# Own-key maxima packed into full banks, exponent floors moved to ScalarE, and a new planned order of instructions

## The chip, the cores and the metric

One NeuronCore of a Trainium2 chip runs the whole program. The metric is device time in microseconds (us) of one launch. The kernel before takes 598.94 us, the median of 3 runs (597.7 to 599.84). Its engines are TensorE (PE in the profile, PEld for its weight loads), VectorE (DVE), ScalarE (ACT), GpSimd (POOL) and SyncE (SP), which issues DMAs.

## The reference

A transformer block on x of 2048 rows by 128 columns: layer norm, then attention and a quantised feed-forward layer side by side, both added to x.

```python
xn = _layernorm(x, axis=-1)
# attention: 16 heads of 8 columns
scores = jnp.einsum('bhqd,bhkd->bhqk', q, k) * scaling
scores = scores + _power_law_mask(S, scores.dtype)[None, None]
attn = jax.nn.softmax(scores, axis=-1)
out = jnp.einsum('bhqk,bhkd->bhqd', attn, v)
# feed-forward: fp4_linear quantises both operands in blocks of 16 to 0, .5, 1, 1.5, 2, 3, 4, 6
h = jax.nn.silu(fp4_linear(x, w_gate)) * fp4_linear(x, w_up)
return fp4_linear(h, w_down)
```

The mask lets query i see key j where j - i >= 0, and weighs it by 1 / (j - i + 1). So a query sees its own position and all later ones.

## The kernel before

**Tiling.** The 2048 positions are 4 groups of 512 (`GROUPS = [3, 2, 0, 1]`, `GQ = 512`), each 4 tiles of 128. A unit is one group of queries with four heads, so there are 16 units, numbered 0 to 15 in the order of the groups. Every unit is computed twice over.

**First pass, the maxima.** For each unit TensorE forms scores with queries on the partitions (item `max`, lines L1425 and, for the triangle where key equals query block, L1428), and VectorE reduces each bank of PSUM to a row maximum (L1240). For keys of a later group a bank is full (512 columns). For the unit's own group ("own keys") query tile a sees 512, 384, 256 or 128 columns, so its four tiles times four heads make 16 banks and 16 reductions, most of them not full. There are 640 such items. When a unit's maxima are done VectorE folds them (`parts`, L1251 and L1256), GpSimd splits them into three bf16 parts (`minor`, L900 to L904), TensorE turns them (`rows`, L1436), ScalarE copies them (L1056) and a DMA puts them as extra rows under the queries (L679).

**Second pass, the scores.** TensorE forms the scores again with keys on the partitions, less the maximum (item `st`, L1449 and L1452, 640 of them). ScalarE takes the exponential (L1049). It is then multiplied by the distance weights: either by GpSimd, two heads at once and interleaved in the ring (L895), or by VectorE, one head at a time (L1267). `pair_vec` says which; in the kernel before it names VectorE for 97 of 320 pairs. Then TensorE multiplies by the values for four heads at once (`pv`, L1467; eight instructions in the trace, as fp32 goes in two passes). The ring has 8 pairs.

**Feed-forward.** 16 tiles, spread over the run. ScalarE makes the curve (L1017 to L1026), VectorE does nine steps (`silu`, L1202 to L1226), of which the last is max(exponent, 1) times a rounding constant (L1226); GpSimd quantises in three steps (`quant`, L911 to L915); TensorE turns and multiplies (L1389, L1400).

**What sets the order.** `plan()` plays the kernel through with a cost for every item and writes down, for each engine, the order in which items are taken. This order is then fixed in the program; each engine runs its list from the front and waits on semaphores. A pair goes to VectorE where the plan sees GpSimd more than `POOL_QUEUE` behind. A pair on GpSimd is charged `POOL_START + 2 * n * POOL_COL`, with 220 ns and 2.04 ns a column. Maxima are kept ahead of scores by `lead_at`. On TensorE a maximum has rank 4 while fewer than two are ahead, a score 4.5; the lower rank is taken first.

## Time and profile before

| | |
|---|---|
| median of 3 runs | 598.94 us |
| profiled execution, its own time | 599.36 us |
| span in that profile | 597.6 us |
| busy: PE, DVE, ACT, POOL | 562.5, 547.1, 409.3, 503.2 us |

Busy time is the union of an engine's instructions. On PE it includes the pipeline latency of each matmul, so a PE that is busy 94% may still have room. On VectorE an instruction's record goes on while the next one has already begun, so the step from start to start is what one more instruction costs, and is shorter than its mean duration.

### The profile page before, as it was taken

What the parts mean: (1) busy time and instruction counts of PE and PEld (TensorE: products, weight loads), DVE (VectorE), ACT (ScalarE), POOL (GpSimd) and SP (SyncE); (2) the same over time, 40 slices, a digit from 0 to 9 for tenths busy, and PEclk for the clock granted to TensorE, in tenths of its full rate; (3) what the DMA queues carried; (4) which work ended last, traced back from release to release, by engine and by line L of the source; (5) the groups of instructions that cost most, each with busy time, mean ns of one, the idle gap of its engine ahead of it and who ended that gap; (6) DMA issues with size and microseconds to landing.
All of it is one profiled execution on the core that took longest, in us unless ns stands there. A gap on an engine that the chain in (4) does not pass through costs nothing.

```text
span 597.6 us, 11270 instructions
## 1 busy us (share of the span) xinstructions
PE 562.5 (94%) x3791; PEld 247.5 (41%) x3791; DVE 547.1 (92%) x1165; ACT 409.3 (68%) x868; POOL 503.2 (84%) x409
## 2 busy tenths in 40 slices
PE   5999999999899999999999999999999998999995
PEld 4677844544343434333333333342344343343322
DVE  5999989998999899999999999999998989999672
ACT  4668486675665567766776676767666767677793
POOL 7378888797998889798999989897988889798773
PEclk9999999999998999999999999999999999999999
DMA  7434344010000001000000000000000000000000
GB/s 203 103 104 113 110 99 108 2 74 8 1 3 1 2 1 60 39 1 2 1 1 1 20 1 2 1 2 2 1 2 19 2 0 2 2 0 2 2 2 18
DMA packets 14832, 16.66 MB, mean 28 GB/s; under 512 B 1639, under 2 KB 14216, under 8 KB 14360
## 3 DMA queue, kind: packets, MB, share of 16 engines
q1 hardware_dynamic: 14240, 15.70, 9.5%
q8 instruction: 30, 0.49, 0.3%
q10 hardware_dynamic: 536, 0.26, 0.2%
q14 instruction: 26, 0.21, 0.1%
HBM read 11.75 MB, written 4.01 MB: 26 GB/s over the span
## 4 chain that ended last, share of the span: by engine, by line
PE 53%; DVE 27%; issue 7%; ACT 7%; POOL 5%; POOLq 0%; ACTq 0%; DVEq 0%
PE psum L1467 14%; DVE mxp L1240 13%; PE psum L1425 13%; PE psum L1449 10%; DVE ring L1267 4%; PE psum L1310 3%; POOL ring L895 3%; PE psum L1381 2%; ACT ring L1049 2%; PE psum L1400 2%; PE psum L1428 2%; PE psum L1383 1%; PE psum L1452 1%; DVE psum L1222 1%; DVE xw L1218 1%
## 5 line engine op out<-in xcount | busy, mean ns | idle before, releaser
L895 POOL TENSOR_TENSOR ring<-ring,dist 128x1024 f32<-128x1024 f32 (+3 forms) x223 | 398.6, 1815 | 51.6 <-ACT ring L1049 50.8
L1240 DVE TENSOR_REDUCE mxp<-psum 128x1 f32<-128x512 f32 (+3 forms) x640 | 354.7, 598 | 16.6 <-PE psum L1425 13.9
L1049 ACT ACTIVATE ring<-psum 128x512 f32<-128x512 f32 (+3 forms) x446 | 221.8, 557 | 93.5 <-PE psum L1452 46.8
L1425 PE MATMUL psum<-kop,qop 96*128 96x512 bf16 (+3 forms) x640 | 198.4, 352 | 7.2 <-DVE mxp L1240 3.7
L1449 PE MATMUL psum<-qop,kop 128*128 128x512 bf16 (+3 forms) x640 | 191.2, 349 | 7.4 <-DVE mxp L1240 2.8
L1467 PE MATMUL psum<-ring,vaug 128*32 128x512 f32 (+3 forms) x1280 | 155.3, 556 | 2.5 <-POOL ring L895 1.9
L1267 DVE TENSOR_TENSOR ring<-psum,dist 128x512 f32<-128x512 f32 (+3 forms) x194 | 115.1, 620 | 12.0 <-ACT psum L1049 11.4
L1049 ACT ACTIVATE psum<-psum 128x512 f32<-128x512 f32 (+3 forms) x194 | 99.7, 545 | 31.7 <-PE psum L1449 19.0
L1425 PEld LDWEIGHTS psum<-kop,qop 96*128 96x128 bf16 x640 | 56.5, 97 | 134.6 <-DVE mxp L1240 45.5
L1449 PEld LDWEIGHTS psum<-qop,kop 128*128 128x128 bf16 x640 | 59.3, 97 | 83.6 <-DVE mxp L1240 19.7
L1428 PE MATMUL psum<-tri_q,identb 128*128 128x128 bf16 x256 | 55.9, 220 | 0.0
L1452 PE MATMUL psum<-tri_k,identb 128*128 128x128 bf16 x256 | 52.5, 219 | 0.0
L1467 PEld LDWEIGHTS psum<-ring,vaug 128*32 128x32 f32 x1280 | 25.8, 108 | 48.7 <-issue 47.1
L1428 PEld LDWEIGHTS psum<-tri_q,identb 128*128 128x128 bf16 x256 | 25.2, 99 | 13.5 <-issue 1.9
L1310 PE MATMUL psum<-identf 128*128 128x128 f32 x200 | 30.8, 274 | 0.0
L1452 PEld LDWEIGHTS psum<-tri_k,identb 128*128 128x128 bf16 x256 | 25.1, 98 | 7.7 <-issue 0.3
L1310 PEld LDWEIGHTS psum<-identf 128*128 128x128 f32 x200 | 22.4, 141 | 3.5 <-issue 0.5
L1017 ACT ACTIVATE xw<-psum 128x352 f32<-128x352 f32 x16 | 7.4, 464 | 17.1 <-PE psum L1383 17.1
L911 POOL TENSOR_TENSOR xw<-xw 128x352 f32<-128x352 f32 x16 | 15.1, 942 | 3.6 <-DVE xw L1226 3.5
L1056 ACT ACTIVATE mrow<-psum 12x512 bf16<-12x512 bf16 x16 | 9.3, 581 | 11.9 <-PE psum L1436 11.9
L1400 PE MATMUL psum<-wdT,hT 128*128 128x128 f32 (+1 forms) x96 | 15.2, 296 | 1.7 <-ACT hT L1035 1.6
L913 POOL TENSOR_TENSOR xw<-xw 128x352 f32<-128x352 f32 x16 | 15.0, 938 | 1.3
(134 smaller groups left out, 467.9 us busy)
## 6 DMA issues: line engine op xcount, KB each, us to landing
parts_dram<-qpart SPq DMA_DIRECT2D x18, 128.0 KB, 3.4
kop<-parts_dram SPq DMA_DIRECT2D x6, 384.0 KB
qop<-parts_dram SPq DMA_DIRECT2D x6, 384.0 KB
xin<-_attn_hidden_states_dram SPq DMA_DIRECT2D x4, 256.0 KB, 5.0
ring<-inv_dram SPq DMA_DIRECT2D x1, 1024.0 KB, 5.1
out_dram<-xin SPq DMA_DIRECT2D x4, 256.0 KB, 2.3
qop<-parts_dram SPq DMA_DIRECT2D x3, 288.0 KB
kop<-parts_dram SPq DMA_DIRECT2D x3, 288.0 KB
```

The costliest lines, as they stand in the source:

```text
L895: g_.tensor_tensor(slot(p)[:, 0:n], slot(p)[:, 0:n], both, ALU.mult).then_inc(weighed_pool, 1)
L911: g_.tensor_tensor(v, v, c, ALU.add).then_inc(hq_seq, 1)
L1049: a_.activation(scores if pair_vec[p] else slot(p)[:, 0:n, e % 2], scores, ACT.Exp, scale=SCALE).then_inc(exp_done, 1)
L1240: v_.tensor_reduce(mxp[:, u % 2, 4 * a + j, c - g:c - g + 1], bank(*o)[:, 0:n], AX_X, ALU.max).then_inc(max_used, 1)
L1267: v_.tensor_tensor(slot(p)[:, 0:n, e % 2], bank("st", e)[:, 0:n], weights(d, n), ALU.mult).then_inc(weighed_vec, 1)
L1310: nc.tensor.transpose(psum[:, OUT_BANK, 0:P], identf[:], identf[:])
L1400: ins = mm(down_of(i), hT[0:k, i % 2, m], wdT[0:k, m], start=(m == 0), stop=(m == 2))
L1425: ins = mm(bank(*o)[:, 0:n], qop[0:K_MAX, u // NQ % 2, h, P * a:P * (a + 1)], kop[0:K_MAX, h, k0:k0 + n], start=True, stop=(c != g))
L1428: ins = mm(bank(*o)[:, 0:P], identb[:], tri_q[:], start=False, stop=True)
L1449: ins = mm(bank(*o)[:, 0:n], kop[0:K_ST, h, P * b:P * (b + 1)], qop[0:K_ST, u // NQ % 2, h, 0:n], start=True, stop=(d >= TPG))
L1452: ins = mm(bank(*o)[:, P * d:P * (d + 1)], identb[:], tri_k[:], start=False, stop=True)
L1467: ins = mm(psum[32 * j:32 * j + 32, OUT_BANK, 0:n], vaug[:, b, VC * h:VC * h + 32], slot(2 * s + j // 2)[:, 0:n, j % 2], start=(b == NT - ...
```

## The change

The numbers in the plan change: a pair on GpSimd is charged 140 ns and 1.906 ns a column, an item for the exponent floor stands on ScalarE, and past half of the work (`LEAN_AFTER`) a score takes rank 3.9 on TensorE, ahead of a maximum, as long as the lead is kept. Own keys: query tile 1 of a head (384 columns) shares a bank with tile 3 (128), and tile 2 of one head (256) with tile 2 of the next, so a unit has 10 own-key items, each of 512 columns, and 544 items in all. One reduction then gives four maxima, for which `mxp` grows from 4 to 7 columns a row. The last silu step leaves VectorE; ScalarE does it as a Relu and an Identity with bias. A pair that VectorE weighs now lies in the ring as two plain halves instead of interleaved.

```diff
-SILU_STAGES, FP4_STAGES = 9, 6
+SILU_STAGES, FP4_STAGES = 8, 6
+LEAN_AFTER = 0.5
+NMX = NG + 3
+ROW_OF = [0, 2, 1, 3]
-POOL_COL, POOL_START = 2.04, 220
+POOL_COL, POOL_START = 1.906, 140
+def max_pieces(a, j):
+    if a == 1:
+        return [(1, j), (3, j)]
+    if a == 2:
+        return [(2, j), (2, j + 1)] if j % 2 == 0 else []
+    return [(0, j)] if a == 0 else []
...
-        pool(("quant", i), 2700, [("DVE", ("silu", i, SILU_STAGES - 1))], rank=0)
+        act(("floor", i), F, [("DVE", ("silu", i, SILU_STAGES - 1))], n=2, rank=2)
+        pool(("quant", i), 2700, [("ACT", ("floor", i))], rank=0)
...
-                return 4.5
+                late = work["st"] > LEAN_AFTER * total
+                return 3.9 if late and work["max"] >= lead_at(work["st"]) else 4.5
...
-        mxp = sb("mxp", [P, 2, TPG * 4, NG], F32)
+        mxp = sb("mxp", [P, 2, 4, TPG, NMX], F32)
+        def weighted(p, j, n):
+            if pair_vec[p]:
+                return slot(p).rearrange("p n j -> p (n j)")[:, GQ * j:GQ * j + n]
+            return slot(p)[:, 0:n, j]
...
+                if o[0] == "floor":
+                    i = o[1]
+                    act.wait_ge(silu_seq, SILU_STAGES * (i + 1))
+                    a_.activation(fbuf[:, 1], gate_of(i), ACT.Relu, scale=ROUND, bias=rounds[:, 0:1]).then_inc(floor_seq, 1)
+                    act.wait_ge(floor_seq, i + 1)
+                    a_.activation(fbuf[:, 1], fbuf[:, 1], ACT.Identity, bias=rounds[:, 1:2]).then_inc(fround_ready, 1)
...
-                    if k < SILU_STAGES - 1:
-                        ins.then_inc(silu_seq, 1)
-                    else:
-                        v_.tensor_scalar(c, gate, 1.0, ROUND, ALU.max, ALU.mult).then_inc(fround_ready, 1)
+                    ins.then_inc(silu_seq, 1)
...
-                    v_.tensor_reduce(mxp[:, u % 2, 4 * a + j, c - g:c - g + 1], bank(*o)[:, 0:n],
-                                     AX_X, ALU.max).then_inc(max_used, 1)
+                    if c == g and a:
...
+                        v_.tensor_reduce(into, parts, AX_X, ALU.max).then_inc(max_used, 1)
+                    else:
+                        v_.tensor_reduce(mxp[:, u % 2, j, ROW_OF[a], c - g:c - g + 1], bank(*o),
+                                         AX_X, ALU.max).then_inc(max_used, 1)
...
+                        if u + 2 < len(units) and parts_of(u + 2)[2] < parts_of(u)[2]:
+                            vec.wait_ge(mneg_ready, 2 * u + 2)
+                            v_.memset(mxp[:, s, :, :, NG - 1:NG], NEG)
...
-                    ins = mm(bank(*o)[:, 0:n], qop[0:K_MAX, u // NQ % 2, h, P * a:P * (a + 1)],
-                             kop[0:K_MAX, h, k0:k0 + n], start=True, stop=(c != g))
-                    if c == g:
-                        ins = mm(bank(*o)[:, 0:P], identb[:], tri_q[:], start=False, stop=True)
+                    x0 = 0
+                    for b, jj in max_pieces(a, j) if c == g else [(a, j)]:
+                        k0 = P * (TPG * g + b) if c == g else GQ * c
+                        n = GQ * (c + 1) - k0
+                        ins = mm(bank(*o)[:, x0:x0 + n], qop[0:K_MAX, u // NQ % 2, 4 * hq + jj, P * b:P * (b + 1)],
+                                 kop[0:K_MAX, 4 * hq + jj, k0:k0 + n], start=True, stop=(c != g))
+                        if c == g:
+                            ins = mm(bank(*o)[:, x0:x0 + P], identb[:], tri_q[:], start=False, stop=True)
+                        x0 += n
```

**Scores first.** TensorE at the last scores of unit 10, in the second half of the work (`kop,qop` with 512 or 384 columns is a maximum, `qop,kop` a score, `tri_k` and `tri_q` triangles, `ring,vaug` the product with the values). Before, at about score 380 of 640:

```order
L1449 MATMUL psum<-qop,kop 128x128
L1452 MATMUL psum<-tri_k,identb 128x128
L1425 MATMUL psum<-kop,qop 128x512
L1449 MATMUL psum<-qop,kop 128x128
L1452 MATMUL psum<-tri_k,identb 128x128
L1449 MATMUL psum<-qop,kop 128x128
L1452 MATMUL psum<-tri_k,identb 128x128
L1467 MATMUL psum<-ring,vaug 32x384 x4
L1425 MATMUL psum<-kop,qop 128x512
L1425 MATMUL psum<-kop,qop 128x384
```

The changed order, at about score 370:

```order
L1476 MATMUL psum<-kop,qop 128x512
L1519 MATMUL psum<-ring,vaug 32x512 x4
L1501 MATMUL psum<-qop,kop 128x384
L1504 MATMUL psum<-tri_k,identb 128x128
L1501 MATMUL psum<-qop,kop 128x384
L1504 MATMUL psum<-tri_k,identb 128x128
L1501 MATMUL psum<-qop,kop 128x384
L1504 MATMUL psum<-tri_k,identb 128x128
L1519 MATMUL psum<-ring,vaug 32x512 x4
L1501 MATMUL psum<-qop,kop 128x384
L1504 MATMUL psum<-tri_k,identb 128x128
L1501 MATMUL psum<-qop,kop 128x256
```

Where one or two scores stood between maxima, five scores and two products with the values now stand before the next one.

**The last unit's rows.** TensorE behind the turning of unit 15's maxima (`identb,mpart`). Before, 13 scores of unit 14 follow it before unit 15's first; these are the first of them:

```order
L1436 MATMUL psum<-identb,mpart 12x128 x4
L1449 MATMUL psum<-qop,kop 128x512
L1452 MATMUL psum<-tri_k,identb 128x128
L1449 MATMUL psum<-qop,kop 128x384
L1452 MATMUL psum<-tri_k,identb 128x128
```

In the changed order, down to unit 15's first two scores (the last row):

```order
L1488 MATMUL psum<-identb,mpart 12x128 x4
L1449 MATMUL psum<-wdT,hT 128x128 x3
L1519 MATMUL psum<-ring,vaug 32x512 x4
L1501 MATMUL psum<-qop,kop 128x128
L1504 MATMUL psum<-tri_k,identb 128x128
L1501 MATMUL psum<-qop,kop 128x128
L1504 MATMUL psum<-tri_k,identb 128x128
L1519 MATMUL psum<-ring,vaug 32x512 x4
L1501 MATMUL psum<-qop,kop 128x128
L1504 MATMUL psum<-tri_k,identb 128x128
L1501 MATMUL psum<-qop,kop 128x128
L1504 MATMUL psum<-tri_k,identb 128x128
...
L1519 MATMUL psum<-ring,vaug 32x384 x4
L1519 MATMUL psum<-ring,vaug 32x256 x4
L1501 MATMUL psum<-qop,kop 128x512 x2
```

Four scores and four products stand between the turning and unit 15's first score.

**The floor on ScalarE.** One feed-forward tile in the changed order (`xw<-psum,rounds` and `xw<-xw,rounds` are the new pair):

```order
L1085 ACTIVATE ring<-psum 128x512 x7
L1085 ACTIVATE psum<-psum 128x512 x2
L1085 ACTIVATE ring<-psum 128x512
L1060 ACTIVATE xw<-psum,rounds 128x352
L1062 ACTIVATE xw<-xw,rounds 128x352
L1085 ACTIVATE ring<-psum 128x512
```

The exponentials behind the pair wait with it when VectorE's steps are late.

In numbers of the two orders: maxima 640 before and 544 now; pairs on VectorE 97 and 90 (of 512 columns 71 and 65, of 384 columns 12 and 13, of 256 columns 10 and 5, of 128 columns 4 and 7); up to the last maximum VectorE weighs 156 and 146 heads; from the turning of unit 15's maxima on, TensorE has 61 scores and 52.

## Rows read from the trace of the kernel before

**Rows 1.** The page: busy time of the engines, share of the span, instructions.

```profile
PE 562.5 (94%) x3791; PEld 247.5 (41%) x3791; DVE 547.1 (92%) x1165; ACT 409.3 (68%) x868; POOL 503.2 (84%) x409
```

**Rows 2.** Busy by stretch, columns: stretch, length, PE, PEld, DVE, ACT, POOL, PEclk, DMA.

```profile
0.00:60.00 60.00, 53.10 (x375) 38.84 (x376) 52.53 (x151) 39.98 (x68) 39.32 (x85) 1.00 0.49 131
60.00:553.00 493.00, 473.67 (x3151) 195.67 (x3148) 470.55 (x972) 338.70 (x732) 435.93 (x304) 1.00 0.06 17
553.00:597.60 44.60, 35.70 (x269) 12.95 (x267) 24.00 (x46) 30.66 (x69) 27.91 (x21) 1.00 0.03 7
```

**Rows 3.** Waits within 60 to 553 us: who, on whom, total, times, longest.

```profile
DVE mxp L1240 <- PE psum L1425: 13.9, 19, 1.6
...
POOL ring L895 <- ACT ring L1049: 43.7, 39, 4.3
POOL xw L911 <- DVE xw L1226: 3.5, 5, 1.1
POOL mres L900 <- DVE mpart L1256: 2.0, 5, 0.6
...
PEld psum L1425 <- DVE mxp L1240: 45.0, 72, 0.9
```

**Rows 4.** Groups by shape: VectorE's maxima and a weighing (busy, mean ns | idle before).

```profile
L1240 DVE TENSOR_REDUCE mxp<-psum 128x1 f32<-128x512 f32 x448 | 292.0, 679 | 14.5 <-PE psum L1425 13.9
L1240 DVE TENSOR_REDUCE mxp<-psum 128x1 f32<-128x384 f32 x64 | 34.4, 543 | 0.1
L1240 DVE TENSOR_REDUCE mxp<-psum 128x1 f32<-128x256 f32 x64 | 26.0, 412 | 0.9 <-PE psum L1428 0.8
L1240 DVE TENSOR_REDUCE mxp<-psum 128x1 f32<-128x128 f32 x64 | 17.3, 278 | 1.1 <-PE psum L1428 1.1
L1267 DVE TENSOR_TENSOR ring<-psum,dist 128x512 f32<-128x512 f32 x142 | 93.0, 681 | 10.4 <-ACT psum L1049 10.0
```

**Rows 5.** Timeline of VectorE, 332 to 336 us: start, length of the merged piece.

```profile
332.28 0.51 DVE L1226 TENSOR_SCALAR xw<-psum 128x352 f32<-128x352 f32 x1
332.71 0.68 DVE L1267 TENSOR_TENSOR ring<-psum,dist 128x512 f32<-128x512 f32 x1
333.31 1.87 DVE L1240 TENSOR_REDUCE mxp<-psum 128x1 f32<-128x512 f32 x3
335.10 0.41 DVE L1267 TENSOR_TENSOR ring<-psum,dist 128x256 f32<-128x256 f32 x1
335.43 1.27 DVE L1240 TENSOR_REDUCE mxp<-psum 128x1 f32<-128x512 f32 x2
```

**Rows 6.** One line, L1251: shortest, median, longest ns.

```profile
L1251 DVE TENSOR_REDUCE mneg<-mxp x16: 150/183/210, 34.7 to 552.7; 128x16 f32<-128x16 f32 x4, 128x16 f32<-128x32 f32 x4, 128x16 f32<-128x64 f32 x4, 128x16 f32<-128x48 f32 x4
```

**Rows 7.** Groups by shape: ScalarE's steps most like the new pair.

```profile
L1026 ACT ACTIVATE xw<-xw 128x352 f32<-128x352 f32 x16 | 8.1, 507 | 0.0
...
L1022 ACT ACTIVATE xw<-psum 128x352 f32<-128x352 f32 x16 | 7.5, 470 | 0.0
```

**Rows 8.** Groups by shape: GpSimd's pairs, four widths.

```profile
L895 POOL TENSOR_TENSOR ring<-ring,dist 128x1024 f32<-128x1024 f32 x153 | 323.5, 2139 | 46.6 <-ACT ring L1049 45.9
L895 POOL TENSOR_TENSOR ring<-ring,dist 128x768 f32<-128x768 f32 x20 | 32.7, 1648 | 0.8 <-ACT ring L1049 0.8
L895 POOL TENSOR_TENSOR ring<-ring,dist 128x512 f32<-128x512 f32 x22 | 25.4, 1163 | 0.3 <-ACT ring L1049 0.2
L895 POOL TENSOR_TENSOR ring<-ring,dist 128x256 f32<-128x256 f32 x28 | 18.4, 674 | 4.0 <-ACT ring L1049 3.9
```

**Rows 9.** Timeline of GpSimd, from 412 us.

```profile
412.10 6.33 POOL L895 TENSOR_TENSOR ring<-ring,dist 128x1024 f32<-128x1024 f32 x3 [3.12 <-ACT ring L1049]
```

**Rows 10.** Timeline, all engines, 551 to 563 us, rows of the last unit's maxima.

```profile
551.72 0.69 DVE L1240 TENSOR_REDUCE mxp<-psum 128x1 f32<-128x512 f32 x1
...
554.49 0.59 ACT L1056 ACTIVATE mrow<-psum 12x512 bf16<-12x512 bf16 x1 [0.57 <-PE psum L1436]
...
555.10 1.80 SPq L679 DMA_DIRECT2D qop<-mrow  x3
...
562.94 0.62 ACT L1049 ACTIVATE ring<-psum 128x512 f32<-128x512 f32 x1 [0.80 <-PE psum L1449]
```

**Rows 11.** Timeline of TensorE, products with the values, 546 to 560 us.

```profile
546.44 1.11 PE L1467 MATMUL psum<-ring,vaug 128*32 128x512 f32 x8
```

More of the change, by code:

```diff
@@ L174, in plan @@
     for u, (g, hq) in enumerate(units):
-        for a, j in sorted(((a, j) for a in range(TPG) for j in range(4)), key=lambda o: o[1] if u == 0 else 0):
+        for a, j in sorted(((a, j) for a in range(TPG) for j in range(4)),
+                           key=lambda o: o[1] + (o[0] == 2) if u == 0 else 0):
             if True:
                 for c in range(g, NG):
-                    n = GQ - P * a if c == g else GQ
+                    pieces = max_pieces(a, j) if c == g else [(a, j)]
+                    if not pieces:
+                        continue
                     item = ("max", u, a, j, c)
-                    h = 4 * hq + j
+                    h = 4 * hq + pieces[-1][1]
                     if g == GROUPS[0]:
@@ L189, in plan @@
                         needs.append(("DVE", ("parts", u - 2, 1)))
-                    pe(item, n + (P if c == g else 0), needs, rank=6)
-                    vec(item, n, [("PE", item)], rank=6)
+                    pe(item, GQ + (P * len(pieces) if c == g else 0), needs, rank=6)
+                    vec(item, GQ, [("PE", item)], rank=6)
         for k in range(2):
@@ L382, in take @@
             issued["maxed"] += 1
-            work["max"] += TPG - item[2] if item[4] == units[item[1]][0] else TPG
+            work["max"] += TPG
         seen[(engine, item)] = end
@@ L525, in build @@
         moments = sb("moments", [P, NT, 2], F32)
+        rounds = sb("rounds", [P, 2], F32)
         amax = sb("amax", [P, len(PIECES), SC_COLS], F32)
@@ L583, in build @@
         fp4_scaled = sem("fp4_scaled")
+        rounds_ready = sem("rounds_ready")
+        floor_seq = sem("floor_seq")
         scales_zeroed = sem("scales_zeroed")
@@ L1048, in _ @@
                         act.wait_ge(pv_done, (p - SLOTS) // 2 + 1)
-                    a_.activation(scores if pair_vec[p] else slot(p)[:, 0:n, e % 2], scores,
+                    a_.activation(scores if pair_vec[p] else weighted(p, e % 2, n), scores,
                                   ACT.Exp, scale=SCALE).then_inc(exp_done, 1)
@@ L1266, in _ @@
                         vec.wait_ge(pv_done, (p - SLOTS) // 2 + 1)
-                    v_.tensor_tensor(slot(p)[:, 0:n, e % 2], bank("st", e)[:, 0:n], weights(d, n),
+                    v_.tensor_tensor(weighted(p, e % 2, n), bank("st", e)[:, 0:n], weights(d, n),
                                      ALU.mult).then_inc(weighed_vec, 1)
@@ L1467, in _ @@
                         ins = mm(psum[32 * j:32 * j + 32, OUT_BANK, 0:n], vaug[:, b, VC * h:VC * h + 32],
-                                 slot(2 * s + j // 2)[:, 0:n, j % 2], start=(b == NT - 1), stop=(b == TPG * g))
+                                 weighted(2 * s + j // 2, j % 2, n), start=(b == NT - 1), stop=(b == TPG * g))
                     ins.then_inc(pv_done, 1)
```

30 lines of the change are left out of this document (21 added, 9 removed).

## The prediction, made before the result was known

> **What bounds the kernel now.** I read the busy shares first [rows 1]. TensorE shows 94%, VectorE 92%, GpSimd 84%, ScalarE 68%. The first figure must not be taken at its word, as a matmul's record holds its latency; the waits tell more. So next the stretches [rows 2]: up to 553 us VectorE is busy 470.6 of 493 us (95%), and behind 553 us, when the last maximum is out, only 24 of 44.6. Then who waits for whom [rows 3]: in the 493 us VectorE waits 13.9 us for TensorE's maxima, while TensorE's weight loads wait 45.0 us for VectorE to free a bank. GpSimd waits 43.7 us for exponentials, so it has room. Up to 553 us the bound is VectorE, in order and almost without holes. Behind it comes a tail of 43 us from the copy of unit 15's rows at 554.49 to the end [rows 10], which scores, exponentials and products set and VectorE does not.
>
> **VectorE, part by part.** What one more instruction costs there is the step from start to start, not the duration. From the timeline [rows 5]: three full reductions begin at 333.31 and the next instruction at 335.10, so 0.597 us each; 256 columns take 0.33 (335.10 to 335.43); L1226 with 352 columns 0.43 (332.28 to 332.71). The mean durations fall by 0.133 us for each 128 columns [rows 4], which gives steps of 0.464 for 384 and 0.20 for 128.
> Packing: 64 x (0.464 + 0.33 + 0.20) = 63.6 us of partial reductions become 96 full ones, 57.3 us: -6.3. That four results instead of one cost nothing more is my assumption; if each cost 0.1 us again, the gain would be 0, and below -6.3 there is nothing to be had, since no column goes.
> Floor: 16 x 0.43 = -6.9.
> Folding: L1251 takes 150 ns for 16 numbers and 210 for 64 [rows 6], 1.25 ns each. It now always reads 112 instead of 40 on average: +0.09 us, 32 times (L1256 alike): +2.9. Two small memsets: +0.3.
> Weighings up to the last maximum: 512 columns 116 to 108, 384 columns 18 to 20, 256 columns 14 to 6, 128 columns 8 to 12: -4.8 + 0.9 - 2.6 + 0.8 = -5.7.
> Together -15.7 us. The plain halves in the ring change nothing that I can see: with the interleaved output a weighing of 512 columns takes 681 ns and a reduction with one result 679 [rows 4]; bounds 0 to -1 us for the products that read them.
> The Trainium skill's "VectorE: DVE Perf Modes", section "The DRAIN you can't avoid", says that the next operation does not start before the pipe is empty. By that every instruction would cost its whole duration and packing would save 64 x (0.543 + 0.412 + 0.278) - 96 x 0.679 = 13.7 us, an estimate with that page's rule and durations of rows 4. The timeline speaks against it here, since a full reduction's successor starts 0.08 us before its record ends.
>
> **GpSimd takes over.** A pair of 512 columns steps by (6.33 - 2.14) / 2 = 2.095 us [rows 9]; the other widths, their durations less 0.044, 1.60, 1.12 and 0.63 [rows 8]. It gets 6 more of 512, 1 fewer of 384, 5 more of 256 and 3 fewer of 128: +14.7 us. Up to the last rows it is 12.1 us, and the quantising of tile 15 (2.8 us) now stands before them too: +14.9. In 60 to 553 us GpSimd is busy 435.9, free 57.1: 43.7 waiting for exponentials, 8 for others [rows 3], 5.4 in gaps. If the stretch shrinks to 477.3, it has 26.5 free, 13.4 of which stay, so its waits for exponentials must fall from 43.7 to 13.1.
> Why they should fall: the old plan charges 2.309, 1.787, 1.264 and 0.742 us for the four widths, against real steps of 2.095, 1.60, 1.12 and 0.63. Over 153, 20, 22 and 28 pairs it charges 42.7 us too much, almost exactly what GpSimd waits: the exponentials stand in the order where a slower GpSimd would want them. The new charge of 2.092 us for 512 columns is right. I do not take the whole of it, since three engines now have to fit at over 90%: waits of 19 us, GpSimd ends 6 us behind VectorE's saving: +6. Ends: 0 and the rival below.
>
> **The floor on ScalarE.** Its nearest steps take 470 and 507 ns [rows 7], about 1.0 us with the wait between them, 16 us in all on an engine busy 338.7 of 493 us: hidden. But the chain from VectorE's last step to GpSimd is longer by about 0.5 us, and GpSimd already waits there 5 times, 3.5 us [rows 3]. Queued behind the pair on ScalarE are exponentials, for which GpSimd and VectorE wait in turn. Between 0 and 16 x 0.5 = 8 us; I take +1.5, as two thirds of the tiles had slack.
>
> **TensorE.** As many matmuls and columns as before: 0. Its real load is a product of four heads at about 1.04 us (1.11 with its latency [rows 11]), and it spends 45 us waiting for VectorE [rows 3], time that comes free when banks do.
>
> **The tail.** From the copy at 554.49 unit 15's first exponential comes 8.45 us later, at 562.94, and the end 34.7 us after that [rows 10]. TensorE had 13 scores to do between; it now has four short ones and four products (about 1.04 + 1.04 + 0.8 + 0.6 us) and the down product, some 4.5 us. The three DMAs are issued by 556.90, 2.4 us after the copy's start; their landing isn't in the rows, so the gap is between 2.4 and 8.45 us. I take 5.4, near the work that stands there: -3. What stood there is done earlier, where VectorE bounds. The alternation of pairs in unit 15: 0, between -2 and +2. The start, where loads and the first chain rule: 0, between -2 and +2.
>
> **Sum.** 597.6 - 15.7 + 6 + 1.5 - 3 = 586.4 us of span. The profiled execution took 599.36, 1.8 over its span, which gives 588.2, and it lies 0.4 above the median: 587.8, so 588 us.
>
> **Rivals.**
> 1. GpSimd becomes the bound and keeps its waits. Its stretch is then 450.8 busy + 57.1 free = 507.9 instead of 493: 597.6 + 14.9 + 1.5 - 3 = 611, about 612 us. For it: its work grows while everybody else's shrinks. Against it: an engine that bounds has its supply waiting, and the overcharge accounts for the waits. It turns to a loss when the waits fall by less than 13 of 43.7 us. Chance 0.08.
> 2. GpSimd and VectorE bound in turns: the waits fall by about 15 to 20 us only. 593 to 599 us. Chance 0.17.
> 3. Scores first starve VectorE. In the second half I count, with the steps above, 14 stretches of over 2 us of other work on TensorE between two maxima, against 7 before, and one of them stands in the order shown. At most three maxima are ahead, 1.8 us of VectorE's time. Seven more holes of 1 us: about 595 us. Against it: VectorE has weighings and silu steps in them, and the lead is asked for first. Chance 0.10.
> 4. All is carried over, GpSimd fits: 597.6 - 15.7 - 3 = 578.9 and 1.4 more, 580 us. Chance 0.10. Each instruction at its full duration would end there as well: 7.4 us below my forecast, 580.5 us. Rows 5 speak against that; chance 0.03.
> My own case, 582 to 593 us, has 0.52. The Trainium skill's rule on the drain, above, is the one that would give the 580.5.
>
> **The numbers.** 588 us. Eight in ten lie between 579 and 599 us: below is half of rival 4, above rival 1 and the end of rival 2. This measurement can tell about 0.3% (1.8 us) from no change. Faster by more (below 597.1): 0.83, which is my case, rival 4, and most of 2 and 3. Within: 0.07, the ends of 2 and 3. Slower: 0.10, rival 1 and 0.02 for mishaps of 3.
>
> **What would show it.** Right: VectorE's reductions of 512 columns with four results at about 680 ns and 0.60 apart; no L1226; its last maximum at 538 to 546 us instead of 551.7; GpSimd's wait for exponentials near 20 us and its share at 88 to 90%; unit 15's first exponential about 5 us behind the last copy of rows. Wrong: reductions with four results over 750 ns; VectorE waiting for maxima over 25 us; GpSimd waiting 35 us or more with its last `minor` no earlier than now.

## The result and the profile after

The changed kernel takes 604.79 us (median of 4 runs, 603.11 to 607.01) against 598.43 us for the kernel before: ratio 1.0094 [1.0064, 1.0123]. Forecast were 588 us, with 0.10 for slower. The span in the profile is 603.3 us against 597.6. The page, its busy line (against [rows 1]) and its chain of waits, and below it the chain of the kernel before:

```profile
PE 559.9 (93%) x3791; PEld 250.0 (41%) x3791; DVE 530.7 (88%) x1041; ACT 422.7 (70%) x900; POOL 516.0 (86%) x418
...
PE 47%; POOL 26%; ACT 12%; issue 5%; DVE 4%; DMA 2%; SPq 1%; ACTq 1%; POOLq 0%; DVEq 0%
```

```profile
PE 53%; DVE 27%; issue 7%; ACT 7%; POOL 5%; POOLq 0%; ACTq 0%; DVEq 0%
```

The chain that ended last ran over VectorE for 27% before and over GpSimd for 26% now.

The savings on VectorE are real: 547.1 us have become 530.7, 16.4 less where 15.7 were forecast. By stretch, as [rows 2]:

```profile
0.00:60.00 60.00, 49.49 (x331) 34.95 (x332) 48.18 (x124) 37.15 (x60) 33.72 (x82) 0.97 0.48 127
60.00:553.00 493.00, 471.03 (x3184) 200.24 (x3181) 458.36 (x871) 352.22 (x766) 447.94 (x314) 1.00 0.06 18
553.00:610.00 57.00, 39.35 (x282) 14.82 (x278) 24.18 (x48) 33.36 (x74) 34.38 (x24) 0.93 0.02 6
```

In the first 60 us all four engines do less than before: TensorE 49.5 instead of 53.1, VectorE 48.2 instead of 52.5, GpSimd 33.7 instead of 39.3. The waits within 60 to 553 us, as [rows 3]:

```profile
POOL ring L923 <- ACT ring L1085: 31.1, 27, 3.2
PEld psum L1476 <- DVE mxp L1287: 23.6, 36, 0.9
DVE mxp L1287 <- PE psum L1476: 19.1, 30, 1.9
...
POOL xw L903 <- DVE hT L1198: 5.9, 3, 2.0
...
DVE mxp L1287 <- PE psum L1479: 3.8, 6, 1.3
```

TensorE's weight loads wait 23.6 us for VectorE instead of 45.0, and GpSimd's wait for exponentials falls from 43.7 to 31.1. The waits that were to shrink did shrink, and the kernel still is slower. VectorE by groups (as [rows 4]: busy, mean ns, idle before), then ScalarE's new pair (against [rows 7]):

```profile
L1287 DVE TENSOR_REDUCE mxp<-psum 128x1 f32<-128x512 f32 x448 | 289.8, 678 | 24.5 <-PE psum L1476 19.1 <-PE psum L1479 4.8
L1316 DVE TENSOR_TENSOR ring<-psum,dist 128x512 f32<-128x512 f32 x130 | 84.9, 681 | 15.4 <-ACT psum L1085 14.9
L1285 DVE TENSOR_REDUCE mxp<-psum 128x4 f32<-128x512 f32 x96 | 64.3, 678 | 3.6 <-PE psum L1479 3.4
```

```profile
L1062 ACT ACTIVATE xw<-xw,rounds 128x352 f32<-128x352 f32 x16 | 9.4, 588 | 0.5
L1060 ACT ACTIVATE xw<-psum,rounds 128x352 f32<-128x352 f32 x16 | 8.9, 559 | 1.4 <-DVE psum L1258 1.1
```

A reduction with four results (L1285) takes 678 ns, as long as one with one result. VectorE's timeline shows the step from start to start: 1.20 us for the two at 25.49, 0.60 each.

```profile
25.49 1.28 DVE L1285 TENSOR_REDUCE mxp<-psum 128x4 f32<-128x512 f32 x2
26.69 0.68 DVE L1287 TENSOR_REDUCE mxp<-psum 128x1 f32<-128x512 f32 x1
27.29 0.68 DVE L1285 TENSOR_REDUCE mxp<-psum 128x4 f32<-128x512 f32 x1
```

**Where the time went.** I took the start of the first exponential of each unit from ScalarE's timelines, which sets both runs side by side:

| first exponential of unit | 0 | 1 | 2 | 4 | 8 | 11 | 13 | 15 | end |
|---|---|---|---|---|---|---|---|---|---|
| before | 48.4 | 76.1 | 93.2 | 118.4 | 229.2 | 395.1 | 486.8 | 562.9 | 597.6 |
| after | 50.7 | 86.2 | 104.0 | 130.6 | 239.2 | 402.4 | 489.8 | 567.1 | 603.3 |
| later by | 2.3 | 10.1 | 10.8 | 12.2 | 10.0 | 7.3 | 3.0 | 4.2 | 5.7 |

The whole loss, and more, is made before unit 4. Behind that point the changed kernel needs 472.7 us where the one before needed 479.2. The 2.3 us of the first column may be scatter: over all profiles of this study unit 0's first exponential comes between 47.5 and 52.5 us, and between 47.5 and 52.1 in the eight that share the changed kernel's order. So the table of the experiments counts from there, in two parts: the start up to unit 4's first exponential (79.9 us against 70.0) and the rest. Together they explain 3.4 of the 6.4 us between the medians; the other 3 lie ahead of the first exponential or in scatter, which one profile of a kernel can't tell apart.

TensorE's granted clock goes with that scatter. In the changed kernel TensorE stood idle for 2.16 us before 40.06, waiting for a DMA of `kop`, and shortly after the clock was at half (1.2 GHz) for 3.4 us:

```profile
35.00:41.30 6.30, 4.14 (x34) 3.11 (x32) 5.52 (x12) 3.81 (x10) 2.23 (x2) 1.00 0.25 81
41.30:44.70 3.40, 3.40 (x17) 2.45 (x16) 3.03 (x7) 0.89 (x2) 3.00 (x7) 0.50 0.28 77
```

Of the eight profiles in this order the three with such a fall ahead of unit 0's first exponential (the changed kernel, e9, e11) have it at 50.4 to 52.1 us, the other five at 47.5 to 49.8. Whether the fall delays it, or both follow a late DMA, no run settles. It doesn't make the late start: e7's clock stays at 1.00 throughout, and its start is as long.

**The mechanism of the start.** Unit 1 can't go on until the ring of 8 pairs empties, which takes unit 0's first product with the values. It comes some 26 us behind unit 0's first exponential before and 34 us in the changed kernel. Here is TensorE at that place, before (L1371 turns a chunk of the quantised input, L1467 is the product; it is the timeline, columns start, length):

```profile
61.80 0.61 PE L1371 MATMUL psum<-identf,xw 128*128 128x128 f32 x4
...
70.80 0.60 PE L1371 MATMUL psum<-identf,xw 128*128 128x128 f32 x4
...
74.58 1.10 PE L1467 MATMUL psum<-ring,vaug 128*32 128x512 f32 x8
...
77.30 0.66 PE L1371 MATMUL psum<-identf,xw 128*128 128x128 f32 x4
```

And after (L1420 turns, L1519 is the product), then ScalarE, which has the copy of the turned chunk (L1036) queued ahead of its next exponential:

```profile
78.39 0.63 PE L1420 MATMUL psum<-identf,xw 128*128 128x128 f32 x4 [0.33 <-DVE mxp L1287]
...
84.16 0.63 PE L1420 MATMUL psum<-identf,xw 128*128 128x128 f32 x4 [0.31 <-DVE mxp L1287]
84.71 1.11 PE L1519 MATMUL psum<-ring,vaug 128*32 128x512 f32 x8
```

```profile
84.82 0.60 ACT L1036 ACTIVATE xnT<-psum 128x512 f32<-128x512 f32 x1 [5.17 <-PE psum L1420]
86.23 1.67 ACT L1085 ACTIVATE ring<-psum 128x512 f32<-128x512 f32 x3 [0.82 <-PE psum L1504]
```

In both orders two turns stand ahead of the first product. A turn needs the quantised chunk from GpSimd, which waits for VectorE's six steps on each piece of the input (the row L903 <- L1198 of the waits above, 5.9 us), and a bank of PSUM, which VectorE frees with a reduction. At 84.16 both came within 0.15 us of each other, GpSimd's last step at 84.01 and the reduction, which the profile names, at 84.15. Either way it is VectorE's row. The last of its six steps (L1162, now L1198) on the first two chunks, before:

```profile
52.17 0.68 DVE L1162 TENSOR_SCALAR hT<-psum 128x512 f32<-128x512 f32 x1
...
59.34 0.68 DVE L1162 TENSOR_SCALAR hT<-psum 128x512 f32<-128x512 f32 x1
```

and after:

```profile
73.73 0.68 DVE L1198 TENSOR_SCALAR hT<-psum 128x512 f32<-128x512 f32 x1
...
79.50 0.67 DVE L1198 TENSOR_SCALAR hT<-psum 128x512 f32<-128x512 f32 x1
```

The first chunk is 21.6 us late, the second 20.2. In between VectorE reduces maxima of units 3 and 4. Own keys are now 10 items and not 16, so the plan gets through each unit's maxima with fewer items, and it places maxima of units further ahead where pieces of the input stood. By the order, TensorE now turns the four chunks behind scores 16, 16, 24 and 36, before behind 6, 16, 18 and 27.

The place of the second turn is not what decides. In e7 (below) the first product stands ahead of it, and the start is as long:

```profile
81.33 1.11 PE L1519 MATMUL psum<-ring,vaug 128*32 128x512 f32 x8
82.60 0.63 PE L1420 MATMUL psum<-identf,xw 128*128 128x128 f32 x4 [0.16 <-DVE mxp L1287]
```

What goes with the length of the start is how many maxima VectorE has taken by the first product. The busy time of its reductions up to there, before (L1240) and after (L1285, then L1287):

```profile
0.00:74.58 74.58, 31.88 (x71) 1.00 0.46 126
```

```profile
0.00:84.71 84.71, 19.44 (x30) 0.98 0.47 124
0.00:84.71 84.71, 20.35 (x32) 0.98 0.47 124
```

That is 31.9 against 39.8 us. If the units are taken in turn, 7 of the 71 reductions are unit 4's before, and 22 of the 62 after. The same count for other orders (steps are an estimate from those of rows 5; the product counts from unit 0's first exponential):

| | reductions | their steps, us | first product after | start |
|---|---|---|---|---|
| before | 71 | 29.6 | 26.1 | 70.0 |
| changed | 62 | 37.0 | 34.0 | 79.9 |
| e7_old_charge, e12_packing_floor | 62 | 37.0 | 33.4 | 81.1 |
| e6_heads | 57 | 34.0 | 33.6 | 79.7 |
| e5_fp4_first | 59 | 35.2 | 31.0 | 77.5 |
| g2_held2 | 51 | 30.4 | 29.4 | 77.1 |
| g1_held1 | 47 | 28.1 | 25.7 | 71.4 |

The plan also places the first product behind the last of 200 filling transposes, in every order. Their own time is not what holds it: e8 leaves out half of them, and the product comes no sooner (34.5 us). No run changes the count of maxima alone; that they hold the product back is read from the seven orders and from the turns' waits.

### The profile page after: what moved, and what is told of

Its sections match the earlier page's. It is cut to its first block, busy times and chain, and to the rows that moved or that the text cites. A ratio compares the mean times of both kernels' runs of the same rounds, so it can differ in the third digit from the quotient of the medians.

```text
span 603.3 us, 11188 instructions
## 1 busy us (share of the span) xinstructions
PE 559.9 (93%) x3791; PEld 250.0 (41%) x3791; DVE 530.7 (88%) x1041; ACT 422.7 (70%) x900; POOL 516.0 (86%) x418
## 4 chain that ended last, share of the span: by engine, by line
PE 47%; POOL 26%; ACT 12%; issue 5%; DVE 4%; DMA 2%; SPq 1%; ACTq 1%; POOLq 0%; DVEq 0%
POOL ring L923 20%; PE psum L1519 15%; PE psum L1476 10%; PE psum L1501 10%; ACT ring L1085 4%; PE psum L1449 2%; DMA kop<-parts_dram 2%; PE psum L1430 2%; POOL xw L941 2%; POOL xw L939 2%; POOL xw L943 1%; PE psum L1432 1%; PE psum L1504 1%; DVE mxp L1287 1%; ACT kop L959 1%
## 5 line engine op out<-in xcount | busy, mean ns | idle before, releaser
L923 POOL TENSOR_TENSOR ring<-ring,dist 128x1024 f32<-128x1024 f32 (+3 forms) x230 | 412.4, 1822 | 37.1 <-ACT ring L1085 36.8
L1287 DVE TENSOR_REDUCE mxp<-psum 128x1 f32<-128x512 f32 x448 | 289.8, 678 | 24.5 <-PE psum L1476 19.1
L1085 ACT ACTIVATE ring<-psum 128x512 f32<-128x512 f32 (+3 forms) x460 | 229.1, 562 | 89.7 <-PE psum L1504 43.9
L1476 PE MATMUL psum<-kop,qop 96*128 96x512 bf16 (+3 forms) x640 | 194.3, 351 | 7.3 <-DMA kop<-parts_dram 2.2
L1501 PE MATMUL psum<-qop,kop 128*128 128x512 bf16 (+3 forms) x640 | 188.2, 349 | 4.7 <-DVE ring L1316 1.6
L1519 PE MATMUL psum<-ring,vaug 128*32 128x512 f32 (+3 forms) x1280 | 156.5, 555 | 8.8 <-POOL ring L923 7.1
L1316 DVE TENSOR_TENSOR ring<-psum,dist 128x512 f32<-128x512 f32 (+3 forms) x180 | 105.0, 616 | 19.6 <-ACT psum L1085 18.9
L1476 PEld LDWEIGHTS psum<-kop,qop 96*128 96x128 bf16 x640 | 58.8, 98 | 104.2 <-DVE mxp L1287 23.6
L1085 ACT ACTIVATE psum<-psum 128x512 f32<-128x512 f32 (+3 forms) x180 | 89.7, 542 | 10.8 <-PE psum L1504 5.3
L1285 DVE TENSOR_REDUCE mxp<-psum 128x4 f32<-128x512 f32 x96 | 64.3, 678 | 3.6 <-PE psum L1479 3.4
L1504 PE MATMUL psum<-tri_k,identb 128*128 128x128 bf16 x256 | 52.1, 218 | 0.0
L1519 PEld LDWEIGHTS psum<-ring,vaug 128*32 128x32 f32 x1280 | 26.4, 108 | 57.5 <-issue 55.6
L1479 PE MATMUL psum<-tri_q,identb 128*128 128x128 bf16 x256 | 48.2, 221 | 0.0
L941 POOL TENSOR_TENSOR xw<-xw 128x352 f32<-128x352 f32 x16 | 14.9, 930 | 1.3
L1449 PE MATMUL psum<-wdT,hT 128*128 128x128 f32 (+1 forms) x96 | 14.9, 291 | 1.0 <-ACT hT L1071 0.9
```

The lines of the kernel that those rows point to most:

```text
L923: g_.tensor_tensor(slot(p)[:, 0:n], slot(p)[:, 0:n], both, ALU.mult).then_inc(weighed_pool, 1)
L1085: a_.activation(scores if pair_vec[p] else weighted(p, e % 2, n), scores, ACT.Exp, scale=SCALE).then_inc(exp_done, 1)
L1285: v_.tensor_reduce(into, parts, AX_X, ALU.max).then_inc(max_used, 1)
L1287: v_.tensor_reduce(mxp[:, u % 2, j, ROW_OF[a], c - g:c - g + 1], bank(*o), AX_X, ALU.max).then_inc(max_used, 1)
L1316: v_.tensor_tensor(weighted(p, e % 2, n), bank("st", e)[:, 0:n], weights(d, n), ALU.mult).then_inc(weighed_vec, 1)
L1476: ins = mm(bank(*o)[:, x0:x0 + n], qop[0:K_MAX, u // NQ % 2, 4 * hq + jj, P * b:P * (b + 1)], kop[0:K_MAX, 4 * hq + jj, k0:k0 + n], start= ...
```

## The experiments

Each kernel was timed in 3 rounds beside the kernel before, whose own median was 598.1 to 599.4 us in these series; the ratio is to the one beside it. e2, e3, e9, f2 and f4 leave a part of the computation out. "Start" is from the first exponential of unit 0 to that of unit 4 in its profile, "rest" from there to the end of the span.

| kernel | median us | ratio to before | start | rest |
|---|---|---|---|---|
| before | 598.43 | 1 | 70.0 | 479.2 |
| changed | 604.79 | 1.0094 [1.0064, 1.0123] | 79.9 | 472.7 |
| e1_interleaved | 605.60 | 1.0106 [1.0079, 1.0132] | 80.0 | 473.7 |
| e2_pool_short | 599.90 | 1.0030 [1.0011, 1.0049] | 79.9 | 468.3 |
| e3_dve_short | 604.00 | 1.0084 [1.0054, 1.0114] | 78.9 | 473.3 |
| e4_no_lean | 614.69 | 1.0273 [1.0246, 1.0300] | 79.9 | 481.4 |
| e5_fp4_first | 598.05 | 0.9989 [0.9973, 1.0004] | 77.5 | 469.4 |
| e6_heads | 605.37 | 1.0100 [1.0075, 1.0126] | 79.7 | 476.0 |
| e7_old_charge | 607.01 | 1.0126 [1.0096, 1.0155] | 81.1 | 473.4 |
| e8_half_fill | 602.92 | 1.0075 [1.0046, 1.0103] | 80.4 | 473.6 |
| e9_both_short | 595.40 | 0.9946 [0.9929, 0.9963] | 78.9 | 464.3 |
| e10_floor_vec | 604.49 | 1.0105 [1.0085, 1.0125] | 79.9 | 473.4 |
| e11_unpacked | 605.71 | 1.0120 [1.0090, 1.0149] | 80.1 | 473.3 |
| e12_packing_floor | 611.96 | 1.0215 [1.0196, 1.0235] | 81.1 | 478.5 |
| f1_new_charge | 600.67 | 1.0032 [1.0019, 1.0045] | 70.9 | 479.6 |
| f2_dve_short | 593.72 | 0.9924 [0.9907, 0.9942] | 69.8 | 472.0 |
| f4_pe_short | 571.27 | 0.9543 [0.9521, 0.9565] | 67.3 | 453.5 |
| f5_lean | 606.10 | 1.0118 [1.0094, 1.0142] | 69.9 | 484.3 |
| g1_held1 | 602.33 | 1.0056 [1.0035, 1.0076] | 71.4 | 475.7 |
| g2_held2 | 604.01 | 1.0096 [1.0072, 1.0120] | 77.1 | 475.3 |

### Which engine bounds: work taken away in a fixed order

**f2_dve_short**, the kernel before.

```diff
-  v_.tensor_reduce(..., bank(*o)[:, 0:n],
+  v_.tensor_reduce(..., bank(*o)[:, 0:P if c > g else n],
```

> The kernel before, with each reduction of a later group's bank reading its first 128 of 512 columns (so most row maxima are wrong), in the same order: some 384 reductions shortened by about 0.4 us each, 150 us off VectorE. If VectorE bounded the kernel before, as the prediction's first step says, this gives back tens of us: 565 to 585. If the order of TensorE and the ring bound it, and VectorE only seemed to be what was waited for (the theory now), it gives little, as in the changed kernel (604.8 to 604.0): 592 to 598.

VectorE's busy time fell from 547.1 to 419.2 us, the kernel by 4.4 (from 598.12 beside it). The page's busy line and the longest wait in 60 to 553 us:

```profile
PE 557.1 (94%) x3791; PEld 249.0 (42%) x3791; DVE 419.2 (71%) x1165; ACT 407.6 (69%) x868; POOL 502.7 (85%) x409
...
DVE mxp L1240 <- PE psum L1425: 59.0, 79, 3.0
```

VectorE is now free over a quarter of the time and waits 59.0 us for maxima instead of 13.9 [rows 3]. GpSimd's wait for exponentials hardly moved (42.0 against 43.7). So VectorE's work on later groups' maxima did not bound the kernel before, though it was 95% busy. The run doesn't reach the start: between 50 and 85 us it took only 2.4 of the 128 us away (34.1 to 31.7 us busy), and e3 below 2.0. The Trainium skill ("Perfetto Trace Analysis", section "Identifying the Most-Contended Engine") advises to take the engine with the highest occupancy and optimise it first, with a warning that TensorE's is no fair measure. By that rule VectorE, at 92%, comes ahead of GpSimd and ScalarE here, and the run speaks against it: 128 us less work there were worth 4.4 us.

**f4_pe_short**, the same, and the matmuls of these maxima shortened as well.

```diff
-  n = GQ * (c + 1) - k0
+  n = GQ * (c + 1) - k0 if c == g else P
```

> The kernel before, in its own order, with the maxima of later groups computed and reduced over 128 of 512 columns (wrong maxima): some 384 matmuls of 0.22 us become 0.06, about 60 us off TensorE, beside the cut on VectorE that alone gave 593.7. If TensorE's work is what is left as the bound, 545 to 565. If the bound is the order itself, the hand-overs from scores to exponentials to weighings to products, with room on every engine, 585 to 592.

```profile
PE 501.3 (88%) x3740; PEld 237.0 (42%) x3791; DVE 411.9 (72%) x1165; ACT 405.0 (71%) x868; POOL 501.2 (88%) x409
```

TensorE's busy time is 56 us less; 50 of its score records are missing from this trace, and the maxima's own matmuls of 512 and 128 columns (L1425) fell by 61 us (171.2 to 110.3). It gave 22 us more (593.7 to 571.3), between the two ranges: 0.4 us a microsecond, against 0.03 on VectorE. TensorE is nearest to the bound, and not alone. This price holds with VectorE's work cut as well; no run shortens TensorE's alone.

**e3_dve_short, e2_pool_short, e9_both_short**, the changed kernel.

```diff
# e3
-  v_.tensor_reduce(..., bank(*o),
+  v_.tensor_reduce(..., bank(*o)[:, 0:P] if c > g else bank(*o),
# e2
-  g_.tensor_tensor(v, v, c, ALU.add)
+  g_.tensor_tensor(v[:, 0:16], v[:, 0:16], c[:, 0:16], ALU.add)
-  g_.tensor_tensor(v, v, c, ALU.subtract)
+  g_.tensor_tensor(v[:, 0:16], v[:, 0:16], c[:, 0:16], ALU.subtract)
# e9: both
```

> The changed kernel in its own order; VectorE's reductions of keys of a later group read 128 of 512 columns (this part of the computation is left out, so the maxima are not the true ones). That takes 384 x 0.4 = 154 us off VectorE's 520. If VectorE still bounds the changed kernel, the time falls by tens of us. If GpSimd and the fixed order bound it, it falls by under 15 us, and GpSimd's wait for exponentials falls towards 10 us.

> The changed kernel in its own order; the first two of GpSimd's three quantising steps of the feed-forward tiles work on 16 of 352 columns (this part of the computation is left out). That takes about 32 x 0.8 = 25 us off GpSimd and nothing off any other engine. If GpSimd bounds the whole run, the time falls by some 20 us or more, to 580 to 585. If it bounds by stretches, by 8 to 15. If the order of the start or VectorE bounds, by less than 4.

> The changed kernel with both cuts at once: the later groups' reductions read 128 of 512 columns (wrong maxima), and two of GpSimd's three quantising steps work on 16 of 352 columns (wrong output). Alone they gave 0.8 and 5 us. If each engine merely stands in for the other as the last one, together they give far more than the sum: 585 or less. If what is left is TensorE's own order and ScalarE, they give about the sum: 597 to 600.

VectorE gave 0.8 us for 132, which is inside the noise, GpSimd 4.9 us for 21 (its busy time is 494.7 instead of 516.0), both together 9.4. That is between the two ranges: more than the sum of 5.7, though hardly by more than the intervals, and far from 585. So the two may stand in for each other a little, and neither bounds. GpSimd's quantising costs 0.23 us a microsecond; its pairs weren't priced in a fixed order.

### The parts of the change in the changed order

**e10_floor_vec, e11_unpacked, e1_interleaved**: each takes one part back and keeps the order of all engines.

```diff
# e10: the floor as one operation on VectorE behind the eighth step, none on ScalarE
+  v_.tensor_scalar(c, gate, 1.0, ROUND, ALU.max, ALU.mult).then_inc(fround_ready, 1)
# e11: one reduction per piece of an own-key bank
-  v_.tensor_reduce(into, parts, AX_X, ALU.max).then_inc(max_used, 1)
+  for b, jj in max_pieces(a, j):
+      ins = v_.tensor_reduce(mxp[:, u % 2, jj, ROW_OF[b], ...], bank(*o)[:, x0:x1], AX_X, ALU.max)
# e1: VectorE's pairs interleaved again
-  if pair_vec[p]:
-      return slot(p).rearrange("p n j -> p (n j)")[:, GQ * j:GQ * j + n]
```

> The changed kernel in its own order, with the exponent floor back on VectorE as one operation of 352 columns behind the eighth step, and nothing for it on ScalarE. The prediction charged the floor's way through ScalarE 1.5 us; the traces show 15 pairs of 1.08 us in ScalarE's row. If it matters, 602 to 603; if neither engine bounds in the place, 604 to 606, and VectorE's 0.44 us x15 more cost nothing.

> The changed kernel in its own order and layout, with the four results of an own-key bank taken by separate reductions (2 or 3 to a bank, 192 where there were 96). By the rows this puts back the 6.3 us of VectorE time that packing saved. If packing is worth its full price, 611; if VectorE has spare time in this order (its cut by 154 us gave 0.8), 604.5 to 606, and a packing worth nothing here.

> The changed kernel in its own order, but a pair weighed by VectorE lies interleaved in the ring, as before the change. If the plain halves cost something (a slower write, or a slower read by the products), the time falls below the changed kernel's 604.8 us, by up to 6 us. If they are free, as I predicted, it stays within 2 us of 604.8.

604.5, 605.7 and 605.6 us against 604.8, with rests of 473.4, 473.3 and 473.7. Each of the three parts by itself is worth nothing that can be told, neither the floor nor 96 reductions fewer nor the layout. What is left as the difference between the kernels is the order.

### The planner's two new rules

**e4_no_lean** (no scores first) and **e7_old_charge** (the old charge for GpSimd), the changed kernel.

```diff
-LEAN_AFTER = 0.5
+LEAN_AFTER = 9
# e7
-POOL_COL, POOL_START = 1.906, 140
+POOL_COL, POOL_START = 2.04, 220
```

> The changed kernel planned anew without scores first in the second half; nothing else of the plan's numbers changes, and the order up to half of the work is the same. If scores first costs, by starving VectorE, the time falls to 598 or less. If it helps GpSimd to its exponentials, it rises to 608 or more. If the loss is that of the first 130 us, where the changed kernel stands 12 us behind, the time stays at 602 to 607 and the first 130 us are unchanged.

> The changed kernel planned anew with the old charge for a pair on GpSimd (2.04 ns a column and 220 ns). Order and start are the same up to the rows of unit 3; then 12 more pairs go to VectorE and none of GpSimd's slack is planned away. If the charge that fits exactly is what costs, the time falls to 595 or less, as the start alone would then leave 12 us less VectorE's savings. If the charge was worth something, it rises above 606. If the start makes the whole loss, it stays at 602 to 607.

**f5_lean** (scores first alone) and **f1_new_charge** (the new charge alone), the kernel before; **e12_packing_floor**, the changed kernel without both rules.

```diff
# f5
-  return 4.5
+  return 3.9 if work["st"] > 0.5 * total and work["max"] >= lead_at(work["st"]) else 4.5
# f1
-POOL_COL, POOL_START = 2.04, 220
+POOL_COL, POOL_START = 1.906, 140
```

> The kernel before, with scores first in TensorE's second half and nothing else of the change; its order up to unit 8 stays as it was. In the changed kernel scores first was worth 10 us (614.7 without it). Theory now (the start alone carries the loss, the rest of the change gains): 589 to 594. Rival (scores first only repairs what the new charge spoils): 597 to 601.

> The kernel before with the new charge for GpSimd alone: 15 us off VectorE and 26 us onto GpSimd. If VectorE bounded the kernel, 588 to 593. If neither engine does and GpSimd's lateness costs as much as its cut gave (25 us for 5), 600 to 606.

> Packed maxima and the floor on ScalarE as in the changed kernel, but with the old charge for GpSimd and no scores first: VectorE carries 4 us less than before (13 us of savings, less the weighings that the old charge gives it), GpSimd 12 us less. The theory (packing replans the start, where units' own-key maxima now come sooner and push the quantising pieces back, +12 us, and the saved VectorE time is worth little): 605 to 612. Rival (the planner's two new rules carry the loss, packing and floor are gains): 590 to 597.

Together with before and the changed kernel these seven form a table, medians in us:

| | old charge | new charge | old charge, scores first | both |
|---|---|---|---|---|
| before | 598.4 | 600.7 | 606.1 | not run |
| packing and floor | 612.0 | 614.7 | 607.0 | 604.8 |

- Packing and floor with the old planner's rules cost 13 us, of which 11.1 are in the start. All kernels of the lower row have a start of 80 to 81 us, all of the upper one of 70 to 71. It is these that replan the start, and the new rules don't touch it. No run has packing without the floor, but the floor's first instruction comes at 135.74 us, behind the first exponential of unit 4, so the start is packing's.
- The new charge costs 2 to 3 us without scores first, and with them seems to give 2 (the intervals overlap). It moves work to GpSimd (busy 526.8 us in f1), whose microseconds are dearer than VectorE's by e2 and e3.
- Scores first gives 5 and 10 us in the lower row and costs 7 in the upper one. My expectation for f5 had neither. Its profile loses the time between unit 11 and unit 15 (175.0 us against 167.8), with more waits of TensorE for VectorE: `PEld L1449 <- DVE` is 25.2 us in 60 to 553 us, before 19.7. Why the sign differs I haven't settled.

### Mending the start

**e5_fp4_first**, the changed kernel, with VectorE's pieces of the input ranked ahead of the maxima.

```diff
-FP4_RANK = 6.5
+FP4_RANK = 3.9
-HELD_RANK, HELD_FREE = 5.5, 3
+HELD_RANK, HELD_FREE = 3.9, 3
```

> The changed kernel planned anew, with the quantising of x and the weights taken on VectorE ahead of the maxima, so that the turning of the first quantised chunk stands on TensorE behind 5 scores as before the change, and not behind 16. If the late start of the scores (unit 1 at 86 us instead of 76) makes the loss, unit 1's first score comes at 78 us or earlier and the time falls to 594 to 599. If the order behind the start makes it, the start is mended and the time stays at 602 or more.

598.05 us, 6.7 less than the changed kernel and level with the one before. The first turn is back behind 5 scores, at 61.97 us. The second is not early (78.33), and the first product comes at 80.10 us instead of 84.71; the last row is the third turn:

```profile
78.33 0.63 PE L1420 MATMUL psum<-identf,xw 128*128 128x128 f32 x4 [0.75 <-DVE mxp L1287]
...
80.10 1.11 PE L1519 MATMUL psum<-ring,vaug 128*32 128x512 f32 x8
...
84.12 0.63 PE L1420 MATMUL psum<-identf,xw 128*128 128x128 f32 x4
```

Only 2.4 us of the 6.7 are in the start, though, 3.3 in the rest. The time met the expectation and its condition did not: unit 1's first exponential comes at 81.6, not by 78. So e5 doesn't show that a mended start brings the time back.

**g1_held1, g2_held2**: the same with one or two free banks asked for instead of three.

```diff
-HELD_RANK, HELD_FREE = 3.9, 3
+HELD_RANK, HELD_FREE = 3.9, 1   # g2: 2
```

> The changed kernel with the input's quantising pieces ranked ahead of the maxima, as in the run that gave 598.05, and allowed to take a bank when only one is free instead of three. TensorE then turns the quantised input behind scores 2, 9, 16 and 24 instead of 16, 16, 24 and 36 (5, 16, 20 and 28 in that run). If the start's order carries the loss, unit 4's first exponential comes at 118 to 123 us and the kernel takes 590 to 595. If banks held by the pieces starve the maxima, 598 to 603.

> The same with two free banks asked for: turns behind scores 3, 12, 16 and 24. By the theory of the start 591 to 597, by the rival 598 to 603.

g1 brings the start back (71.4 us; unit 4's first exponential at 123.2, of which 51.8 lie before unit 0's). Three turns now stand ahead of the first product, and both the second turn and the product come early:

```profile
65.92 0.66 PE L1420 MATMUL psum<-identf,xw 128*128 128x128 f32 x4
...
73.74 0.60 PE L1420 MATMUL psum<-identf,xw 128*128 128x128 f32 x4
77.51 1.11 PE L1519 MATMUL psum<-ring,vaug 128*32 128x512 f32 x8
```

Yet its median is 602.3 us: the rest takes 475.7 instead of 469.4. So the order of the start explains the start, and the total still hangs on the order behind it, which every new number in the plan writes anew: in the eight different orders of the packed kernel the rest took 469.4 to 481.4 us. (One or two of these us can be the clock's at the end, see below.) The theory "mend the start and the rest's gain remains" fell with g1.

**e6_heads, e8_half_fill**: two waits or loads of the start, one each.

```diff
# e6: heads' DMA planned later
-DMA_ROWS, DMA_LATE_ROWS, DMA_HEADS, DMA_CHUNK, DMA_NEXT = 6000, 4500, 8000, 20000, 13000
+DMA_ROWS, DMA_LATE_ROWS, DMA_HEADS, DMA_CHUNK, DMA_NEXT = 6000, 4500, 11500, 20000, 13000
# e8: every second filling transpose left out
-  if o[0] == "warm":
+  if o[0] == "warm" and o[1] % 2 == 0:
```

> The changed kernel planned anew with the time that the loads of unit 1's and 2's heads really take (11.5 us a part instead of 8), since TensorE stands up to 40 us waiting for them in the changed kernel and did not before. If that wait is the loss, the time falls by the 4 us of it, to about 600. If it is hidden, it stays within 2 us of 604.8.

> The changed kernel in its own order, with every second of the 200 filling transposes on TensorE left out. They stand before the first product with the values, and scores from unit 1 on need it for room in the ring. If TensorE's work in the start sets unit 1's first score, it comes 8 to 10 us earlier and the time falls by as much, to 595 to 598. If it waits for the quantised chunk (VectorE, GpSimd), the start and the time stay as they are, within 2 us.

Neither shortens the start (79.7 and 80.4 us). In e6 TensorE's wait for `kop` (2.16 us before 40.06 in the changed kernel) is gone from that place, and still 57 reductions stand ahead of the first product, so the start stays.

## Why the prediction was wrong

**The first step failed: "Up to 553 us the bound is VectorE, in order and almost without holes."** I read it from a share of 95% and from waits on VectorE [rows 2, 3]. A share of 95% says that an engine is seldom idle, not that the end waits for it: f2 took 128 us from it for a gain of 4.4. The 45.0 us that TensorE's weight loads waited for VectorE were no gain in store either. In the changed kernel they are 23.6, and it is slower; in f2 they are 29.6, and it gained 4.4. From this step came the sign of the sum, -15.7 us. Priced by the runs in a fixed order, 0.01 (e3) to 0.03 us (f2) a microsecond, it was worth half a microsecond at most. The size of the saving was right (16.4 us of busy time); its worth was not. These prices say nothing of the first 85 us, where VectorE's row does seem to hold back the rest, by the order of its items.

**The second failure: "The start, where loads and the first chain rule: 0, between -2 and +2."** It was +10. I had shown two places of the new order, in the second half and at the end, and put the start at nothing without reading its order, where packing changes the count of items and so everything that is placed between them. The 2 us were no bound from rows. VectorE now takes 22 maxima of unit 4 instead of 7 ahead of the first product, and the first chunk of the input 21.6 us later.

**What was right in size.** The packing: I assumed four results at no extra cost, and it is 678 ns, 0.60 apart. (The bound beside it was off: 96 x 0.1 us would have made a loss of 3.3 us, not 0.) The floor: estimated 470 and 507 ns, measured 559 and 588, the pair 1.17 us from start to end instead of 1.0, and its price of 1.5 us was 0 within the noise (e10). The copy of unit 15's rows to its first exponential: forecast 5.4 us, measured 5.7, against 8.45 [rows 10]:

```profile
561.38 0.57 ACT L1092 ACTIVATE mrow<-psum 12x512 bf16<-12x512 bf16 x1
...
567.05 1.14 ACT L1085 ACTIVATE ring<-psum 128x512 f32<-128x512 f32 x2 [1.19 <-PE psum L1501]
```

But from there the end is 36.2 us away and not 34.7, so the tail shrank by 1.2 us (43.1 to 41.9 from the copy) and not by 3. TensorE's clock took 0.9 of that: it fell to half (1.2 GHz) at 597.7, after a stretch of 7.7 us with 4.17 busy, and the last eight matmuls took 2.05 us. Before, at a clock of 1.00, they took 1.13. In order: the changed kernel's clock by stretch, its last matmuls, and those of the kernel before:

```profile
590.00:597.70 7.70, 4.17 (x46) 2.03 (x43) 1.04 (x4) 3.04 (x9) 3.16 (x4) 1.00 0.00 0
597.70:603.30 5.60, 2.05 (x8) 1.78 (x8) 0.69 (x1) 0.00 (x0) 0.00 (x0) 0.50 0.16 47
```

```profile
597.80 2.05 PE L1542 MATMUL psum<-wp,xw 128*128 128x128 f32 x8 [0.87 <-ACT xw L1104]
```

```profile
592.98 1.13 PE L1490 MATMUL psum<-wp,xw 128*128 128x128 f32 x8 [0.87 <-ACT xw L1068]
```

The last maximum is done at 556.2, not between 538 and 546:

```profile
554.29 1.88 DVE L1287 TENSOR_REDUCE mxp<-psum 128x1 f32<-128x512 f32 x3
```

**The signs.** Those named for being wrong all stayed away: reductions at 678 ns (over 750), VectorE's waits for maxima at 23.9 us (over 25), GpSimd's for exponentials at 31.1 (35 or more). They looked at engines, and none at the order of the start.

**GpSimd.** "Its waits for exponentials must fall from 43.7 to 13.1", taken as 19, are 31.1. I counted its extra work as +6 behind VectorE's saving. As VectorE's saving gave no time back, nothing stands against the price of that work. By e2 it is 0.23 x 14.9 us, some 3.4 us, an estimate that takes pairs to cost what quantising does. f1 speaks for less: there GpSimd has 23.6 us more and the kernel is 2 us slower, in a new order.

**TensorE.** "As many matmuls and columns as before: 0" is right, but I read its 45 us of waits as time "that comes free when banks do", and left it at that. What it does is worth 0.4 us a microsecond (f4), the dearest work that was priced, and the change takes none of it away.

**The rivals.** Rival 3 had scores first at a loss; in the changed kernel it gives 10 us, in the one before it costs 7. The measured 604.8 lies between the end of rival 2 (599) and rival 1 (612). Rival 1 turns to a loss when GpSimd's waits fall by less than 13 us, and they fell by 12.6, which by its own account is hardly a loss. None of the rivals had the place where it was lost. A rival worth naming would have been: packing replans the start, and no engine's saving pays for it.
